# Mamba transposes among the projections, token-major routing, two-scan first gates

## The reference, cut to what matters

```python
# gate, per channel: a_t = a_{t-1} * decay + ekv_t, forward and reversed
num = nf + nb - ekv + euk * vf
den = df + db - ek + euk
base = sigmoid(r) * (num / maximum(den, 1e-08))
# Mamba2: projections, 4-tap convolution, then per chunk and head
Y_diag = einsum('bcgls,bgHcls,bcsgHp->bclgHp', CB, Lmat, xdt)
states = einsum('bcsgn,bgHcs,bcsgHp->bcgHpn', Bc, decay_states, xdt)
```

## Time and profile before

| | |
|---|---|
| median of 3 runs | 2736.46 us (2734.57 to 2736.86) |
| the profiled execution | 2736.24 us, its span 2734.5 us |
| mean granted clock of TensorE | 0.923 |
| busy: TensorE, VectorE, ScalarE, GpSimd | 2261.7, 1916.4, 932.6, 674.8 us |

### The profile page before, as it was taken

How to read it: one execution, slowest core, us unless ns; L and a number is a source line. 1 busy time by engine, 2 the same in 40 slices (tenths; PEclk the granted TensorE clock), 3 DMA queues, 4 the chain that set the end, 5 groups by cost and what they waited for, 6 DMA issues and landing times.

```text
span 2734.5 us, 32797 instructions
## 1 busy us (share of the span) xinstructions
PE 2261.7 (83%) x10127; PEld 1697.0 (62%) x10144; DVE 1916.4 (70%) x2899; ACT 932.6 (34%) x1907; POOL 674.8 (25%) x536
## 2 busy tenths in 40 slices
PE   0677977967967489988955789999999999899998
PEld 0335444444443267866744668887888877688887
DVE  8868878788788666566654556877877876566665
ACT  2133234333333223233312334444444443322222
POOL 2333433333332343334341101212212211000000
PEclk9988988989978689989976889999999999999999
DMA  4000000000002433234223100001001101110001
GB/s 194 16 31 31 16 31 31 31 15 31 31 15 77 167 104 107 77 138 146 70 99 112 31 16 31 16 16 39 16 16 39 31 31 35 39 35 23 23 12 62
DMA packets 50532, 142.15 MB, mean 52 GB/s; under 512 B 4800, under 2 KB 4800, under 8 KB 46096
## 3 DMA queue, kind: packets, MB, share of 16 engines
q1 hardware_dynamic: 32336, 93.03, 9.6%
q10 hardware_dynamic: 12432, 29.66, 2.9%
q0 software_dynamic: 5680, 18.62, 2.3%
HBM read 106.95 MB, written 34.34 MB: 52 GB/s over the span
## 4 chain that ended last, share of the span: by engine, by line
PE 39%; issue 32%; POOL 9%; DVE 8%; POOLq 5%; ACT 3%; DMA 2%; ACTq 1%; SPq 0%; DVEq 0%
PE bank L337 8%; PE bank L339 8%; PE bank L338 8%; PE bank L2047 3%; PE bank L2048 3%; PE bank L2049 3%; PE bank L2006 3%; POOLq L508 2%; POOL g_v L516 2%; POOL g_v L509 2%; PE bank L2042 1%; POOLq L534 1%; POOLq L520 1%; POOLq L531 1%; DVE rinv L1691 1%
## 5 line engine op out<-in xcount | busy, mean ns | idle before, releaser
L1906 PE MATMUL bank<-um,w_in 128*128 128x512 f32 x576 | 259.6, 611 | 10.8 <-DVE lm L1310 10.8
L1906 PEld LDWEIGHTS bank<-um,w_in 128*128 128x128 f32 x576 | 111.4, 196 | 153.3 <-issue 136.3
L337 PE MATMUL bank<-u_hi,aw_hi 128*128 (+1 forms) x384 | 158.6, 413 | 9.7 <-issue 9.4
L1054 ACT ACTIVATE probs<-bank,nmx 128x128 f32<-128x128 f32 (+3 forms) x256 | 131.7, 527 | 91.1 <-DVE nmx L1694 91.1
L338 PE MATMUL bank<-u_lo,aw_hi 128*128 (+1 forms) x384 | 152.0, 396 | 0.0
L339 PE MATMUL bank<-u_hi,aw_lo 128*128 (+1 forms) x384 | 152.0, 396 | 0.0
L1061 ACT ACTIVATE pt_hi<-bank 128x512 fp32r<-128x512 f32 (+1 forms) x192 | 94.0, 526 | 160.9 <-PE bank L2006 160.9
L337 PE MATMUL bank<-u_hi,fw_hi 128*128 128x512 f32 x352 | 136.9, 389 | 0.0
L338 PE MATMUL bank<-u_lo,fw_hi 128*128 128x512 f32 x352 | 136.9, 389 | 0.0
L339 PE MATMUL bank<-u_hi,fw_lo 128*128 128x512 f32 x352 | 136.9, 389 | 0.0
L2006 PE MATMUL bank<-ident,probs 128*128 128x128 f32 x640 | 97.1, 284 | 47.2 <-DVE pt_lo L1709 27.2
(11 more groups left out here) (357 smaller groups left out, 6251.4 us busy)
## 6 DMA issues: line engine op xcount, KB each, us to landing
m_stage<-in_moe SPq DMA_DIRECT2D x24, 1024.0 KB, 6.3
y_slot<-m_o ACTq DMA_DIRECT2D x39, 256.0 KB, 2.8
g_v<-in_fT SPq DMA_DIRECT2D x18, 512.0 KB, 3.5
gates<-g_v SPq DMA_DIRECT2D x18, 512.0 KB, 2.8
f_stage<-in_ffn SPq DMA_DIRECT2D x11, 768.0 KB, 4.3
u_g<-gates SPq DMA_DIRECT2D x8, 1024.0 KB, 5.7
aw_in<-in_att SPq DMA_DIRECT2D x4, 1280.0 KB, 6.0
w_in<-in_w_in ACTq DMA_DIRECT2D x1, 4640.0 KB, 17.0
```

What stands on the lines that cost most here:

```text
L337: nc.tensor.matmul(out, hi_w, hi_x, start=start, stop=False)
L1054: A(probs[:, h % 2, PR_AT[qb]:PR_AT[qb] + w], S_[bk][:, c0:c0 + w], ACT.Exp, bias=nmx[:, h % 2, qb:qb + 1], scale=SCALE, accum_out=rsum[:, ...
L1906: mm = M(dst[:], w_in[:, k, c0:c0 + P], um[:, k, :], start=(k == 0), stop=(k == KC - 1))
```

## The change

Three changes come together. **First gates:** tiles are made two at a time in the form that the later pairs have (clamp, edge factor, one forward and one backward scan for each of two rows, one reciprocal for two tiles), with twelve products and sums on GpSimd; the pair (0, 0) moves behind `mamba_input(0)`. ScalarE and TensorE start without waiting for all masks, and the load of `gw` is issued after the gate inputs. **Mamba:** cumulative sums come after chunk 1; z chunks start two chunks later; the B/C transposes (`from_conv`) and the transposes of one channel tile for all four blocks (`to_tokens`) are issued between the projections; VectorE multiplies each channel (`weighted`, into `state` and `xdt`), the gate steps move by a place, and six state matmuls go into six banks. In the pair loop e2 comes after the exponentials. **Routing:** `moe_input` is called between the last sums; each token tile has its transposes and its logits matmuls with tokens on partitions, three banks for the tiles; the last sequence's tanh and product are made in quarters; the first expert's load is issued by ScalarE, its subtraction is VectorE's, after routing; the index table comes before other tables.

```diff
-        XB = (R0, R1), (YD, YO)
+        XB = YD, YO
         RB = (R0, R1), PJ
-        LGT, UT, LGP = bank[0:2], bank[2:6], bank[6]
+        SB = (R0, R1), PJ, (YD, YO)
+        UT, LGP = bank[4:7], bank[7]
...
             odd = eng is nc.vector
-            if not odd:
-                eng.wait_ge(lgt_done, b + 1)
-                if b >= 2:
-                    eng.wait_ge(lgt_used, b - 1)
-                nc.scalar.activation(lgT[:, b % 2, :], LGT[b % 2][0:E, :], ACT.Copy).then_inc(lgt_copied, 1)
...
+            sp.dma_start(condT_s[:], condT).then_inc(loaded, 16)
             sp.dma_start(rows[:], rows_d).then_inc(loaded, 16)
-            sp.dma_start(condT_s[:], condT).then_inc(loaded, 16)
+            for i in range(2):
+                sp.dma_start(pre_values(i), fT[2 * i:2 * i + 2].rearrange("o p t -> p o t")).then_inc(pre_in, 16)
...
-                if a == KC:
-                    stage(0)
...
+            def pre_product(i, t):
+                v, e, ek, eu = pre_tile(i, t)
+                pool.wait_ge(setup_step, PRE_CLAMPED[i, t])
+                combine(e, ek, v, ALU.mult).then_inc(pre_pool, 1)
+            def pre_add(i, t):
+                v, e, ek, eu = pre_tile(i, t)
+                pool.wait_ge(setup_step, PRE_SUMS[i, t])
+                combine(v, v, e, ALU.add).then_inc(pre_pool, 1)
+            pre_product(0, 1)
+            pre_product(1, 0)
+            pre_product(1, 1)
+            pre_add(0, 0)
+            pre_add(0, 1)
+            (v0, _, d0, _), (v1, _, d1, r) = pre_tile(0, 0), pre_tile(0, 1)
+            pool.wait_ge(setup_step, PRE_DENS)
+            combine(r, d0, d1, ALU.mult).then_inc(pre_pool, 1)
+            pool.wait_ge(setup_step, PRE_INVERSE)
+            combine(d1, r, d1, ALU.mult).then_inc(pre_pool, 1)
+            combine(d0, r, d0, ALU.mult).then_inc(pre_pool, 1)
+            pre_add(1, 0)
+            pool.wait_ge(pre_pool, PRE_ADDED[1, 0])
+            combine(um[:, 0, :], v0, d1, ALU.mult).then_inc(pre_pool, 1)
...
-            for p in range(M_PIECES):
-                pool.wait_ge(mw_hi_ready, p + 1)
-                o = slice(p * M_PIECE, (p + 1) * M_PIECE)
-                nc.gpsimd.tensor_tensor(mw[:, 0, 1, o], m_stage[:, o], mw[:, 0, 0, o].bitcast(F32), ALU.subtract).then_inc(w_split, 1)
...
-            act.wait_ge(setup_step, SETUP_STEPS)
-            act.wait_ge(pre_in, 16 * KC)
+            act.wait_ge(setup_step, N_GATES)
+            act.wait_ge(pre_in, 32)
...
+                    if q == 1:
+                        act.wait_ge(cs_neg, b + 1)
                         A(w2e[:], w2[:], ACT.Exp).then_inc(w_exp, 1)
                         A(cdec[:], SM[:, 128:128 + NB], ACT.Exp).then_inc(w_exp, 1)
+                        A(csT[0:HEADS_M, :], EB[0:HEADS_M, :], ACT.Copy).then_inc(ct_hi, 1)
...
+                    if 4 <= q < 4 + TB:
+                        tb = q - 4
+                        act.wait_ge(bc_done, TB * b + tb + 1)
+                        A(b_tok[:, tb, :], SM[:, 192:320], ACT.Copy).then_inc(bc_copied, 1)
+                        A(cb[:, tb, :], SM[:, 320:448], ACT.Copy).then_inc(bc_copied, 1)
...
-                    A(e2[:, j % 2, :], EB[:], ACT.Exp).then_inc(l_done, 1)
                     for hh in range(2):
                         for tb in range(TB):
                             i = tb * HEADS_M + 2 * j + hh
                             r = RB[j % 2][hh][:, tb * P:(tb + 1) * P]
                             A(r, r, ACT.Exp, bias=csn[:, i:i + 1]).then_inc(l_done, 1)
-                    if j in (4, 5):
-                        gate(mamba_pair(b, 3), j - 4)
+                    if j >= 2:
+                        act.wait_ge(y_done, PAIRS * b + j - 1)
+                    A(e2[:, j % 2, :], EB[:], ACT.Exp).then_inc(l_done, 1)
+                    if j == 0:
+                        gate(mamba_pair(b, 2), 1)
+                    if j in (5, 6):
+                        gate(mamba_pair(b, 3), j - 5)
...
+            def last_sequence(m):
+                act.wait_ge(x_added, KC * (BATCH - 1) + m + 1)
+                A(tx_moe[:, m, :], XT[:, m, tok(BATCH - 1)], ACT.Tanh, scale=0.5).then_inc(last_tanh, 1)
+            act.wait_ge(u_ready, FIRST + 2 * BATCH - 1)
+            for m in range(KC - 1):
+                last_sequence(m)
+            token_copies(act, 0)
+            last_sequence(KC - 1)
+            for p in range(M_PIECES):
+                o = slice(p * M_PIECE, (p + 1) * M_PIECE)
+                act.dma_start(m_stage[:, o], moe_d[0][:, o]).then_inc(m_staged[p], 16)
+            for b in range(1, BATCH):
...
+            def pre_clamp(i, t):
+                dve.wait_ge(setup_act, 4 + 2 * (2 * i + t + 1))
+                ek = pre_tile(i, t)[2]
+                setup.inc(V.tensor_scalar(ek, ek, EXP30, pre_col(inflow, i, t), ALU.min, ALU.mult))
...
+            def pre_forward(i, t):
+                d = pre_col(decay, i, t).to_broadcast([P, T])
+                for x in pre_tile(i, t)[2:0:-1]:
+                    if x is not None:
+                        setup.inc(V.tensor_tensor_scan(x, d, x, 0.0, ALU.mult, ALU.add))
...
+            pre_clamp(0, 0)
+            setup.wait()
+            v, e, ek, _ = pre_tile(0, 0)
+            setup.inc(V.tensor_tensor(e, ek, v, ALU.mult))
+            setup.wait()
+            pre_value(0, 0)
+            pre_clamp(0, 1)
+            assert setup.n == PRE_CLAMPED[0, 1], setup.n - SETUP_STEPS
+            setup.wait()
+            pre_forward(0, 0)
+            pre_clamp(1, 0)
+            assert setup.n == PRE_CLAMPED[1, 0], setup.n - SETUP_STEPS
+            setup.wait()
+            pre_edge(0, 0)
+            setup.wait()
+            pre_backward(0, 0)
...
+            scans((0, 0), 0)
+            scans((0, 0), 1)
+            dens((0, 0))
...
+                def weighted(ch):
+                    dve.wait_ge(x_transposed, XC * b + ch + 1)
+                    for dst, n, factor in ((state, TB - 1, dts), (xdt, TB, dt_t)):
+                        out = dst[:, :, ch * P:(ch + 1) * P].rearrange("p a (h d) -> p a h d", h=2)
+                        ins = V.tensor_tensor(out, by_token(XB[ch % 2][:], n, ch), of_heads(factor, n, ch), ALU.mult)
+                        if factor is dt_t:
+                            ins.then_inc(xdt_done, 1)
+                        else:
+                            step.inc(ins)
...
+                    elif q > 6:
+                        if q < 9:
+                            scans(second, q - 7)
+                    if q >= 5:
+                        weighted(q - 5)
                 step.wait()
+                dens(second)
+                weighted(5)
+                inverse(second)
+                weighted(6)
+                weighted(7)
...
+                for half in range(2):
+                    for tb in range(TB - 1):
+                        state_sum(tb, half)
+                clamp(mamba_pair(b, 2), 0)
...
-                with dve.If(b == BATCH - 1):
-                    for nxt in range(BATCH - 1):
-                        moe_input(nxt)
                 dens(fourth)
-                step.wait()
-                dve.wait_ge(u_ready, FIRST + b + 2)
                 for m in range(KC):
-                    if m == KC - 1:
+                    if m < BATCH - 1:
+                        with dve.If(b == BATCH - 1):
+                            moe_input(m)
+                    else:
                         inverse(fourth)
+                    if m == 0:
+                        step.wait()
+                        dve.wait_ge(u_ready, FIRST + b + 2)
...
+            token_copies(dve, 0)
+            dve.wait_ge(g_fetched[BATCH - 1], 16)
+            for m in range(KC):
+                dve.wait_ge(last_tanh, m + 1)
+                u = uf1[:, BATCH - 1, m, :]
+                V.scalar_tensor_tensor(u, tx_moe[:, m, :], 1.0, u, ALU.add, ALU.mult).then_inc(last_u, 1)
+            for b in range(1, BATCH):
...
+            split_lo(0, 0, (0,))
             select(0, 0)
             select(1, 1)
+            split_lo(0, 0, (1,))
             u_lo_split(0)
+            split_lo(0, 0, (2,))
...
+                def from_conv(tb):
+                    o = slice(tb * P, (tb + 1) * P)
+                    if tb:
+                        pe.wait_ge(bc_copied, 2 * (TB * b + tb))
+                    else:
+                        pe.wait_ge(act_ready, N_CONV * b + 2)
+                        pe.wait_ge(w_exp, 2 * (b + 1))
+                    nc.tensor.transpose(SM[:, 192:320], bT[:, o], ident[:])
+                    M(SM[:, 320:448], bT[:, o], cT[:, o], start=True, stop=True).then_inc(bc_done, 1)
+                def to_tokens(ch):
+                    pe.wait_ge(act_ready, N_CONV * b + ch + 3)
+                    if ch >= 2:
+                        pe.wait_ge(xdt_done, XC * b + ch - 1)
+                    for tb in range(TB):
```

(41 more changed lines are left out.)

375 lines of the change are left out of this document (173 added, 202 removed).

## The result

The changed kernel takes 2695.53 us (median of 4 runs, 2692.69 to 2698.4), the kernel before 2736.66 in the same session: ratio 0.9852, 95% interval [0.9838, 0.9867]. That is 41 us less where 84.5 were forecast; 2695.5 lies 3.5 us above the range that ended at 2692. The sign was right, the size half.

What follows compares the result with a forecast made beforehand. VectorE bounds setup and routing; TensorE and VectorE alternate before the pair loop. Gains of 13.5 + 47 + 24 = 84.5 us from 2736.2 give 2652 us; own range 2640 to 2675 (0.64), whole range 2620 to 2692.

Steps and rivals of the forecast that it cites:

- First gates: Setup to sequence 0's dt chain on VectorE: two-scan gate tiles start that chain 13.5 us earlier (bounds 8 and 18).
- Mamba: The four Mamba iterations: each gains a net 11.8 us, 47 us in all (bounds 30 and 60).
- Routing: From w_out's end through routing: token copies, weight subtraction and index table together gain 24 us (bounds 17 and 29).
- D to Y0: VectorE's first dt instruction to the first pair's matmuls, per iteration: 93 us instead of 104.7, 11.7 gained.
- rival (a): Projections: TensorE waits in order on VectorE's products and ScalarE's copies; iterations gain 2 to 3 us; 2689 us, chance 0.14.
- The last reciprocal and channels 6 and 7 are what is late next: Before the state matmuls: VectorE finishes these 80.3 us after its first dt instruction; TensorE waits some 4 us.
- The clamps of the fourth pair: End of the pair loop: placed after the last y, they delay the scans and next dt chain by 1.3 us.
- the term for the token copies: Behind w_out: token tiles of 1.4 to 1.9 us end at 908 instead of about 917, 11 us gained (6 to 15).
- On the queues: Token stores: with weights on ScalarE's queue, a store's 11.16 us wait behind weights shrinks to a few us.
- (b): State stretch: no lower clock as TensorE no longer alternates; 16 us gained per iteration, 2632 us, chance 0.17.
- (c): Projections: waits hold TensorE at 1.2 GHz; slower, 2740 to 2780 us for six to nine slow chunks, chance 0.03.
- (d): Whole kernel: the waits only move and nothing is measured, chance 0.02.

Runs made afterwards that it cites:

- wide logits: Changed kernel with token stores first and early token copies, plus logits as four matmuls per sequence with 512 tokens moving, as before the change: 2682.43 us, 0.9808.

## Why the prediction was half right

**First gates: right.** The clamp started at 12.0 (13 forecast), VectorE took 56.8 us to the end of the `um` product (53.3), the way to D 21.3 (20.2): 11.4 us by the marks, 8.5 [5.5, 11.8] alone, for 13.5 with bounds of 8 and 18. Of what is missing, 3.5 us are contention: the price was right and the count was not. Sixteen GpSimd instructions ran in the 56.8 us (the x16 of the first stretch), the twelve new ones and four products of the pair (0, 0) that the sum left out. By the prediction's own sum the undisturbed work is 43.7 us, so VectorE lost 13.1, which is 0.8 for each of sixteen. The other 1.1 us are waits for GpSimd on the way to D, 2.38 and 1.46 where the prediction had 2.5. The clamps of the pair gate show the contention:

```profile
51.88 1.48 DVE L434 TENSOR_SCALAR g_s<-g_s,inflow 128x512 f32<-128x512 f32 x1
53.28 1.48 DVE L435 TENSOR_SCALAR g_eu<-g_eu 128x512 f32<-128x512 f32 x1
...
83.17 0.49 DVE L471 TENSOR_SCALAR g_s<-g_eu,oscale 128x512 f32<-128x512 f32 x1 [2.38 <-POOL g_v L496]
```

The first two are 1.0 us longer than alone (0.48 and 0.42). By the Trainium skill (SBUF — State Buffer, Who interferes with whom) a `tensor_scalar` in a two-port mode and a GpSimd instruction exclude each other, and whoever issues first holds the shared ports for its whole length. These rows agree in direction. GpSimd lost time as well: its sixteen instructions were busy 27.5 us, and one takes 1.27 where nothing disturbs it, so both engines together lost some 20 us, the length of the sixteen. VectorE's share stayed at 0.8 for each, and the 6 us less that the prediction drew from that rule did not come.

**Mamba: the failed step, 47 forecast, 18.9 measured.** Two terms, read from the run of this part alone.
- D to Y0: 11.7 forecast, 7.7 measured (103.2 and 95.5), 16 us in four iterations. 1.5 of the 4.0 is the reference: I priced the second sequence, 104.7, and the four have a mean of 103.2. The rest is ScalarE. The prediction had TensorE waiting for taps and products. ScalarE's copies of B and C it named in rival (a) and priced at nothing, and they now stood behind the second pair's exponentials: two table loads of 1.28 and 2.4 us of exponentials ahead of a copy that TensorE needs in order. The wait of 3.88 drags 2.1 us of slow records behind it. Without both the projections end at D+71.8, two under the forecast D+74: the same sum was too high elsewhere, which hid part of this miss. It is rival (a)'s mechanism, TensorE in order waiting within the projections, on the engine that this rival named second.
- "The last reciprocal and channels 6 and 7 are what is late next": right, and priced. The prediction had "a wait of some 4 us" there and a slow row behind it, and the wait was 4.02. This is no part of the miss. What it did not ask is whether the wait could go: the run with the pair one chunk earlier has Y0 at D+84.2.
- The clamps of the fourth pair: 1.3 forecast; 3.4 measured in three iterations and 7.6 behind the last w_out, 12.6 us more in all, so that by the marks the two terms make up the 28 us that are missing (28.6; about 3 of them are the shift between marks told above). I counted the two clamps. I did not follow what waits for them (GpSimd's four products, then the scans) nor that the last two products then run beside the scans. At j = 6 they stood in VectorE's wait for the last pair and cost next to nothing. With that one edit undone the kernel gains 21 us.

**Routing: 24 forecast, 11.2 measured.** The chain was right: 13 forecast, 12.4 measured, no instruction of 4 us left, L1627 at 0.29. The second failed step is the term for the token copies, 11 us gained: alone they lose 4, and in the changed kernel the stretch loses 9.6 together with the Mamba tail. Two reasons are shown. The stores stood behind a gate store in SyncE's order (7 us by the marks). And the price of 1.4 us a tile came from rows at the high clock, where 2.45 us at the low one applied (granted clock 0.56, and 0.86 with wide logits). A third is argued only: with both cured the DMA engines are busy 0.83 of the time at 302 GB/s in the fifteen microseconds shown, and the one run that moved a load moved the wait with it. The prediction walked the step past the weights' queue, and not past SyncE's own waits for GpSimd's result and memset; the sign it named, first copies that stall on ScalarE, is there with 13.79 us. The first gather, forecast some 25 us nearer to w_out's end, is 3.4 nearer (76.1 and 72.7).

On the queues: the store that waited 11.16 us stood behind 3 MB of weights on its own queue. By the Trainium skill (DMA: Bandwidth & Descriptors, Queues, rings and completion order) the rings take turns, so the wait should shrink. With the weights on the other queue the first store, issued at 863.9, released the copy at 871.0: 7 us. These are two single stores beside different loads, and they agree in direction. The engines still have to move the same bytes, and they were busy throughout in those 7 us, at 344 GB/s.

**The rivals.** (b) did not come: the state matmuls ran at 8.02 us for twelve records, inside the forecast's 5.1 to 10.2. (c) did not: the projections of an iteration had a mean clock of 0.91, with one hitch. (a) came in part: an iteration gained 6 by the marks, between its 2 to 3 and the 12 of the forecast. Its 2689 was the nearest of all the numbers, and that is luck: it had 10 us for Mamba where 19 came, and 24 for routing where 11 came. (d) is out, since 41 us are far from nothing. One slip stands in (b): it takes 27 us for routing where the part itself has 24, so its 2632 should be 2635.

## What to carry to other kernels

When work is moved in an in-order engine's program, list for every engine what now stands ahead of the instruction that someone waits for: here four exponentials ahead of a 0.3 us copy cost 22 us, two clamps behind a y 21, a gate store ahead of the token stores 7 by the marks. Price short matmuls at the clock that the row before them has, and a wait on TensorE at the wait plus the slower records behind it. And undo a change edit by edit even where it is faster: the three parts gave 41 us, and 75 more lay in the placement of a few calls and in the form of one matmul.

## What the runs showed of the hardware

- TensorE stayed at 1.2 GHz (granted clock 0.50) through the 22 us of token tiles from 871.7 to 893.9 in the changed kernel, in which its records follow one another without a gap: transposes of 128 columns and 8-column matmuls, weight loads busy 22.1 of 22.2 us. It had fallen at the wait of 4.66 us ahead of the fourth tile (four transposes in 0.63 us before it, 1.11 behind it). With wide logits in the same place the clock also fell, at a wait of 3.64 us, and was back within the next eight wide records (the sixteen transposes behind them take 2.00 us); that stretch had 0.86. In the Mamba rows shown, the records behind a wait of 4 us were slow (9.14 for 7.03, 7.47 for 5.42).
- VectorE and GpSimd slowed each other: sixteen GpSimd instructions of 512 columns beside VectorE's work from 12 to 68.8 us cost VectorE 13 us, 0.8 each, and were themselves busy 27.5 us where sixteen times 1.27 is 20.3, so that both losses together are about the length of the sixteen (times on GpSimd are rough).
- A table load on ScalarE took 1.28 us, and the exponential behind it began at once (324.23 + 1.28, and 325.52). The Trainium skill (ScalarE: Activation LUTs, What ACT_TABLE_LOAD costs) adds a drain of about 1.4 us to each; no row here shows it, and the two loads cost 2.6 us together.
- The kernel before does not repeat exactly: its iterations, the same instructions, took 193.8 to 197.3 us from D to D, with D to Y0 between 101.2 and 104.8. The sequence that one prices is a sample.
